# A semaphore for every sum of a group and every step of a block, places unpacked without an AND, and PSUM operands in the setup of a four-layer graph network

## The reference

```
h = max(layernorm(x), 0); x = x + L0(h, weights)   # messages scaled by sqrt(softmax over incoming * softmax over outgoing)
h = max(layernorm(x), 0); x = x + L1(h, beta)      # two AGNN layers, each:
    nh  = h / max(norm(h), 1e-12)
    e   = beta * sum(nh[src] * nh[dst], -1)
    p   = segment_softmax(e, dst)
    h   = relu(segment_sum(h[src] * p[:, None], dst))
h = max(layernorm(x), 0); x = x + L2(h, weight)    # sum over 16 edge types of mask * (h[src] @ w_r), summed by dst
h = max(layernorm(x), 0); x = x + L3(h, ...)       # segment_sum by (receiver * 32 + type), then 32 matrices, mean, self weight, bias
```

## Time and profile before

| | us |
|---|---|
| median of 3 runs (16609.46 to 16620.77) | 16613.94 |
| the profiled execution | 16705.54 |
| its span | 16703.7 |
| busy in it: POOL | 9403.8 (56%) |
| PE, weight load | 7120.6 (43%), 6075.7 (36%) |
| DVE | 6471.3 (39%) |
| ACT | 2680.9 (16%) |
| POOL's gathers: 8310 of 943 ns | 7839.0 |

### The profile page before, as it was taken

One profiled execution on the slowest core, in us unless ns is written; L12 is line 12 of the kernel. 1 busy time (PEld: TensorE's weight loads), 2 busy tenths in 40 slices (PEclk: granted clock), 3 DMA queues, 4 the chain that ended last, 5 costly groups with the idle time before them and its releaser, 6 DMA issues. The chain is left out here.

```text
span 16703.7 us, 167845 instructions
## 1 busy us (share of the span) xinstructions
PE 7120.6 (43%) x35085; PEld 6075.7 (36%) x35140; DVE 6471.3 (39%) x18639; ACT 2680.9 (16%) x7299; POOL 9403.8 (56%) x9933
## 2 busy tenths in 40 slices
PE   4311112222222566666656666665333334333333
PEld 1100001222222555555555555554323233223323
DVE  3322224333333455555545555554222223222222
ACT  0000000000000333333333333333000000000000
POOL 5476763655555555555545555554656656566666
PEclk5555555555555555555555555555555555555555
DMA  1000001111111111111121111112111112111111
GB/s 29 3 5 5 5 4 44 22 21 21 21 21 19 37 36 39 36 36 39 36 38 42 46 42 42 43 42 37 39 38 40 40 38 44 31 23 23 23 23 22
DMA packets 429667, 499.79 MB, mean 30 GB/s; under 512 B 235856, under 2 KB 245584, under 8 KB 417584
## 3 DMA queue, kind: packets, MB, share of 16 engines
q0 software_dynamic: 317504, 279.59, 10.7%
q1 hardware_dynamic: 97730, 214.09, 3.8%
q10 hardware_dynamic: 14316, 4.81, 0.1%
HBM read 397.49 MB, written 94.54 MB: 29 GB/s over the span
## 5 line engine op out<-in xcount | busy, mean ns | idle before, releaser
L680 POOL DMA_INDIRECT Z<-table,idx x4986 | 4703.3, 943 | 4326.8 <-issue 1700.3
L1575 PE MATMUL ps<-Z 128*128 128x65 f32 x9972 | 2313.9, 419 | 4972.2 <-DVE pay_d L1367 2504.1
L1575 PEld LDWEIGHTS ps<-Z 128*128 128x128 f32 x9972 | 2189.5, 329 | 5209.0 <-issue 5065.3
L1367 DVE SCALAR_TENSOR_TENSOR pay_d<-pay_d,ps 128x65 f32 x4986 | 1110.2, 223 | 4000.0 <-issue 2976.3
L680 POOL DMA_INDIRECT Z<-table_a,idx x1662 | 1567.8, 943 | 1090.1 <-issue 549.0
L656 POOL DMA_INDIRECT bins_dst<-slot_d x1612 | 1561.5, 969 | 959.4 <-issue 495.7
L680 POOL DMA_INDIRECT Z<-table_b,idx x1662 | 1567.9, 943 | 894.1 <-issue 514.6
L1562 PE MATMUL ps<-Z 128*128 128x65 f32 x6648 | 1532.9, 418 | 275.1 <-DVE pay_d L1214 213.1
L1562 PEld LDWEIGHTS ps<-Z 128*128 128x128 f32 x6648 | 1468.5, 331 | 361.1 <-DVE Z L1202 240.0
L1529 PE MATMUL ps<-pay_d,Z 128*128 x6648 | 1532.9, 421 | 33.2 <-ACT Z L738 31.1
L1529 PEld LDWEIGHTS ps<-pay_d,Z 128*128 128x128 f32 x6648 | 1485.5, 333 | 32.4 <-issue 32.1
(11 more groups left out here) (245 smaller groups left out, 7975.3 us busy)
## 6 DMA issues: line engine op xcount, KB each, us to landing
pay_d<-locals_ SPq DMA_DIRECT2D x92, 1152.0 KB
Z<-table,idx POOLq DMA_INDIRECT x4986
table_b<-pay_d SPq DMA_DIRECT2D x192, 256.0 KB
Z<-table_a,idx POOLq DMA_INDIRECT x1662
Z<-table_b,idx POOLq DMA_INDIRECT x1662
bins_dst<-slot_d POOLq DMA_INDIRECT x1612
table_a<-kept SPq DMA_DIRECT2D x94, 256.0 KB
slot_d<-pay_d SPq DMA_DIRECT2D x62, 91.0 KB
```

Source lines behind the costliest of these rows:

```text
L680: nc.gpsimd.indirect_dma_start(rows[:, at.slot, j, 0:width], None, ps_.table, bass.IndirectOffsetOnAxis(ap=idx[:, at.slot, j:j + 1], axis= ...
L1367: v.scalar_tensor_tensor(out=of_block, in0=of_block, scalar=1.0, in1=p_pair[:, at.two, j * ROW:(j + 1) * ROW], op0=ALU.mult, op1=ALU.add). ...
L1575: last = mm(p_pair[:, at.two, j * ROW:(j + 1) * ROW], hot_d[:, at.three, j, :], given, start=True, stop=True)
```

## The change

1. **A semaphore for each item.** `item_added0` to `item_added5` replace `added`, `part_added`, `sum_added` and `sum_part`. Sum j of group g waits for `item_added[j-1]` to reach `done(e + g)`, the same value for all j.
2. **A semaphore for each step.** `blk_step1` to `blk_step15` replace `blk_step`; the value is `rank.n` plus a constant, the same for steps with the same history.
3. **One count of groups.** `own` is gone; every semaphore of a group counts `e + g` in all passes. Those that only AGNN passes use start at `CREDIT + NG`. `hot_f_direct` is merged into `hot_f_made`.
4. **Places.** `two & 4095` becomes `two - (two >> 12) * 4096`.
5. **Setup.** ACT copies each bf16 part of the weights to PSUM, and DVE subtracts it from there (new waits `weights_cast`, `weights_kept`). In `layer_norm` the factors by row are written to PSUM, and the square takes one operand from PSUM, for which `h` is copied (one more instruction of 3136 elements). PE's local turns wait for `table_made` instead of `x_cleared`, since the same PSUM is used.

```diff
-            one = (two & 4095, two >> 12)[j % 2]
+            one = (two - (two >> 12) * 4096, two >> 12)[j % 2]
...
+        def blk_step(k):
+            return blk_steps[k - 1]
         def step_of(p, rank, k):
-            return rank.n * OPS[p] + (sum(OPS[:p]) * NB + k)
+            return rank.n + (sum(OPS[q] >= k for q in range(p)) * NB + 1)
...
                 def then(rank, k, ins):
-                    ins.then_inc(blk_step, 1)
-                    dve.wait_ge(blk_step, step_of(p, rank, k))
+                    ins.then_inc(blk_step(k), 1)
+                    dve.wait_ge(blk_step(k), step_of(p, rank, k))
...
                         if j == 0:
                             dve.wait_ge(summed, done(e + at.g))
-                            dve.wait_ge(sum_added, done(own + at.g - 1))
+                            dve.wait_ge(added, done(e + at.g - 1))
                         else:
-                            dve.wait_ge(sum_part, (own + at.g) * (ITEMS - 1) + j)
+                            dve.wait_ge(item_added[j - 1], done(e + at.g))
                         of_block = acc[:, bass.ds(place_at(at, j), ROW)]
                         v.scalar_tensor_tensor(out=of_block, in0=of_block, scalar=1.0, in1=p_pair[:, at.two, j * ROW:(j + 1) * ROW],
-                                               op0=ALU.mult, op1=ALU.add).then_inc(sum_added if j == ITEMS - 1 else sum_part, 1)
+                                               op0=ALU.mult, op1=ALU.add).then_inc(item_added[j], 1)
...
+            for k in range(2):
+                act.wait_ge(weights_cast, k + 1)
+                nc.scalar.copy(p_cast, w_parts[:, k, :]).then_inc(weights_kept, 1)
...
-                link(v.tensor_scalar(col_a[:, :], col_a[:, :], 1.0 / D, None, ALU.mult))
-                link(v.tensor_tensor(h_sb[:, :, :], x_sb[:, :, :], bc(col_a[:, :]), ALU.subtract))
-                link(v.tensor_tensor(sq[:, :, :], h_sb[:, :, :], h_sb[:, :, :], ALU.mult))
+                link(v.tensor_scalar(p_rows, col_a[:, :], 1.0 / D, None, ALU.mult))
+                link(v.tensor_tensor(h_sb[:, :, :], x_sb[:, :, :], bc(p_rows), ALU.subtract))
+                link(v.tensor_copy(p_h, h_sb[:, :, :]))
+                link(v.tensor_tensor(sq[:, :, :], h_sb[:, :, :], p_h, ALU.mult))
...
-            link(v.tensor_copy(w_parts[:, 0, :], w_f32))
-            link(v.tensor_tensor(w_f32, w_f32, w_parts[:, 0, :], ALU.subtract))
-            link(v.tensor_copy(w_parts[:, 1, :], w_f32))
-            link(v.tensor_tensor(w_parts[0:D, 2, :], w_f32[0:D, :], w_parts[0:D, 1, :], ALU.subtract))
+            for k in range(2):
+                v.tensor_copy(w_parts[:, k, :], w_f32).then_inc(weights_cast, 1)
+                dve.wait_ge(weights_cast, k + 1)
+                dve.wait_ge(weights_kept, k + 1)
+                to = w_f32 if k == 0 else w_parts[0:D, 2, :]
+                rows_of = slice(0, P) if k == 0 else slice(0, D)
+                link(v.tensor_tensor(to, w_f32[rows_of, :], p_cast[rows_of, :], ALU.subtract))
...
-            pe.wait_ge(x_cleared, 1)
+            pe.wait_ge(table_made, 1)
```

More of the change, by code:

```diff
@@ L379, in gnn_program, with __init__ @@
         class Pass:
-            def __init__(self, kind, every, gather, own, column=0, table=None):
+            def __init__(self, kind, every, gather, column=0, table=None):
                 self.p = every
@@ L716, in work @@
             def work(ps_):
[L717 removed]
+                e = ps_.every
                 def rows_wanted(at):
```

162 lines of the change are left out of this document (85 added, 77 removed).

## The result

The changed kernel takes 16,376.9 us (median of 4 runs, 16,371.7 to 16,399.6), the kernel before 16,611.7 (4 runs, 16,548.8 to 16,620.8). The ratio is 0.9869, 95% interval 0.9843 to 0.9895: 1.3% faster, 235 us, where the prediction had 1030. The profiled execution took 16,381.8 us, its span is 16,380.0.

What follows compares the result with a forecast made beforehand. DVE's instruction list was taken to bound edge, plain a and plain b; the AGNN passes' late signal stayed open. -740 - 300 + 10 = -1030 from 16,705.5, less 91.6 above the median, gave 15,584 us; range 14,800 to 16,540.

Steps and rivals of the forecast that it cites:

- The length of DVE's list, not its busy time, sets these three passes.: Edge, plain a, plain b: slow register instructions (0.70 us) put DVE behind and stop POOL by the full ring; 740 us gain.
- a signal of PE that was 10.4 us on the way: AGNN passes: score spreads' last matmul ends 10.4 us before DVE's L1163 stops waiting; cause left open.
- Both accounts: Edge, plain a, plain b: slow stretch charges every instruction (lower, 560 us gain) or register instructions alone (upper, 929 us).
- A term that was left out as below 0.1 us a group: DVE's sums: the fused place of an even item may take longer than an ALU_OP alone, 20 ns at 3 a group.
- The three passes without softmax: Edge, plain a, plain b: fewer DVE instructions save 740 us, the middle of 560 and 929.
- The AGNN passes: Both AGNN passes: shorter DVE and PE lists save 300 us, two thirds of 469 us "issue" idle time; least sure term.
- a forecast of 10: Setup: ACT's two copies and the copy of `h` add 10 to 12 us, taken as 10.
- all is on the path: Setup: the first gather waits for DVE, so the added copies count in full, 10 to 12 us.
- Rival 1: Loop passes: DVE's list is held until POOL's stream ends, whatever its count; 93 us saved, with +10 16,531; chance 0.14.
- Rival 2: All passes: POOL's rests go, 929 us and 1266 us in AGNN, with +10 14,429; chance 0.09.
- Rival 3: First AGNN pass: DVE waits for the late signal every group, one rest each, +928 us; 16,812 in all; chance 0.06.
- Rival 4: Loops: long bodies are loaded again each trip, so mainly the second AGNN pass gains, 93 us; 16,438 in all; chance 0.03.

Runs made afterwards that it cites:

- `e_two_sums`: Changed kernel with the four inner of six sums of a group left out in plain b: 12,802.1 us, 0.9984 of the kernel before.

## Why the prediction was wrong

**The step that failed** is "The length of DVE's list, not its busy time, sets these three passes." What the list did was right, what it was worth was not. Summed over the records, register instructions of DVE that last over 0.6 us (loads from memory left out) had 709, 261, 264, 717 and 750 us in the five passes before, 2701 together, and have 501, 5, 5, 224 and 247 after, 982. That is 1719 us less in DVE's slow stretches, and the passes got 259 us shorter; with the parts undone, in one group, 1079 to 2047 us of them went with times 76 us apart. What POOL waited for instead is PE's signal: in plain b in every rest of both kernels, in plain a through ACT, with a part before the change that did wait for DVE. In the stretches shown it comes 3.4 us (before) and 4.2 us (after) behind the stream's last gather, whether DVE was still behind with its own sums (before) or had been waiting for 14 us (after). Plain b has a rest every 4.1 groups (277 by 68) for 2.9 (277 by 94), but the rests are longer, 5.0 us in the median for 4.2. That a sooner start of PE on each group is what gets one more group into a stream is a reading, not shown.

**What should have been seen.** The earlier trace rows names the releaser of the rest: "remote", not DVE, and a slot of the ring comes free in plain b by PE's sums, not by DVE's. For the earlier trace rows the prediction noted a signal of PE that was 10.4 us on the way, and kept it apart as a matter of the AGNN passes. Had the same been asked of the rest in the earlier trace rows, plain b would have shown it too. Both accounts, 560 and 929 us, were fitted to three passes in which the rests, the counts and the time go up together; a fit of three points by one constant could not tell cause from company. (The upper one has a slip: 1.31 and 1.14 should be 1.30 and 1.12, 922 us in all, which changes nothing.) A term that was left out as below 0.1 us a group, the longer place of an even item, is 0.11 us an item, 0.33 a group, and takes back at full pace what the shorter list gives.

**By the terms.** The three passes without softmax: 740 expected, 145 measured (-9 + 127 + 27). The AGNN passes: 300 expected, 114 measured (12 + 102); there DVE's slow instructions all but vanished and the first pass did not move, so they had not set it. L1163's "remote" idle time, the largest wait of DVE in the first of these passes, was 451.2 us over 81 times before and is 436.7 over 122 after, in the same line's place (L1180); that of L1214 grew from 262.4 to 619.3 (L1231):

```profile
DVE pay_d L1231 <- remote: 619.3, 135, 9.7
DVE ps L1180 <- remote: 436.7, 122, 5.4
DVE pay_d L1231 <- issue: 101.1, 243, 0.9
```

**The setup** came out as expected, by two errors that cancel. From the first cast to the end of the table's product the kernel before took 34.6 us (2665.55 to 2700.17), the changed one 43.9 (2608.38 to 2652.23): +9.2 for a forecast of 10. ACT's copies take 2.78 us instead of the 3.7 worked out from the length of 768; the gap that each leaves on DVE is 2.91; the copy of `h` to PSUM costs 3.43, the upper end; and PSUM operands made none of the subtractions shorter (3.42). That "all is on the path" holds only with stalls; without them this code is done 1100 us before the first gather.

The lines of the changed kernel:

```profile
2608.38 1.79 DVE L1403 CAST weights<-Z 128x3136 bf16<-128x3136 f32 x1 [26.98 <-DMA Z<-in_w_self]
2613.09 3.42 DVE L1408 TENSOR_TENSOR Z<-Z,ps 128x3136 f32<-128x3136 f32 x1 [2.91 <-ACT ps L851]
...
2632.91 3.43 DVE L1132 COPY ps<-Z 128x3136 f32<-128x3136 f32 x1
```

```profile
2610.21 2.78 ACT L851 CAST ps<-weights 128x3136 f32<-128x3136 bf16 x1 [28.75 <-DVE weights L1403]
```

**The rivals.** Rival 1 (the stretch is a length of time) came nearer to the mechanism: it said 83 us, too little, but the signals of PE and SP do come back together about 4 us behind POOL's stream. Its "held up until POOL's stream ends" is too strong, since signals also arrive amid a stream, late. Rival 2 (rests go in all passes) did not happen. Rival 3 (the phase of the first AGNN pass breaks) did not: 136 rests before, 136 after. Rival 4 (loops fetched anew) had 93 us for the second AGNN pass, and it gained 102; but plain a, whose body of 195 instructions the rival leaves out, gained 127, and in three groups the same loops run without any stall. The rule on taken branches in the Trainium skill ("Runtime: NRT & Kernel Launch", "Instruction fetch mechanics"), cited there, is not needed for anything in these traces.

**What stays open.** What brings the stalls; what in the hardware joins POOL's gathers and scatters to the pace of the other engines; whether PE or only its signal is slow; and what keeps the AGNN passes near 10.8 us a group. No run with a still shorter list of DVE fell into a group with stalls (`e_two_sums` fell into one without), PE's instructions were not halved in plain b with stalls, the only pass whose rests all end on its sums, and the changed kernel never ran in one group with its undone parts.

## What to carry to other kernels

When an engine rests, follow the semaphore that ends the rest before pricing the engine that looks slow beside it: a stretch that is slow on one engine may be slow on others too, as here, and shortening one list then turns its "issue" idle time into "remote" idle time (1090 us into 1138 in plain b). A model with one fitted constant needs a point that it could fail on, such as a pass with the same rests and another count. And before instructions are counted for a gain, run the kernel again at another time and place: a program of 16,600 us ran at 12,800 in three groups, and 1.3% became 0.15%.

## What the runs showed of the hardware

- The kernel before takes 12,807 to 12,823 us in three groups and 16,448 to 16,755 in three others (and 16,612 in the first measurement), with the same granted clock of 0.50; in the changed kernel the busy times are the same in both kinds as well. Within a group runs agree to 0.5%. One chip was in both.
- Where there are stalls, while POOL issues gathers one after another, DVE takes 0.70 us for many of its register instructions, SP sees one signal in up to 4.9 us, and in plain b PE's signal ends a rest of POOL 13.1 us (before) and 21.7 us (after) behind PE's modelled end in the median. In the stretches shown all recover 3.3 to 4.2 us behind POOL's last gather. In the other groups none of it shows under the same stream: the signal is 0.25 us behind, at most 0.34.
- With stalls DVE waits long under POOL's indirect scatters as well: it reaches L1122 of the setup at 958 us without stalls and at 2579 with them.
- With stalls a break of 1.4 us on POOL after six gathers keeps plain b on its floor (2389 us for 2382); one of 0.95 us halves the loss above the floor (150 us for 317).
- The register instruction of `two - (two >> 12) * 4096` with the column offset takes DVE 0.21 us, the AND and the offset apart 0.045 and 0.053.
- ScalarE copies 3136 bf16 elements to PSUM in 2.78 us, where 768 elements through another activation took 0.92 us.
